# Experts stage: GpSimd starts a round's four result scatters only after the previous round's have landed

## The reference

```python
x = x + layernorm(attention(layernorm(x)))   # 16 heads of 8, relative position bias, softmax over 1024 keys
x = x + layernorm(ffn(layernorm(x)))         # mixture of experts
# ffn: 64 experts, 8 of them per token (best 4 of 8 groups first), capacity 128 tokens per expert
xe = zeros((E, CAP, H)).at[sorted_e, pos].set(tok_sorted, mode='drop')
h = silu(einsum('ech,efh->ecf', xe, w1)) * einsum('ech,efh->ecf', xe, w3)
ye = einsum('ecf,ehf->ech', h, w2)
out = segment_sum(vals * flat_w[:, None], flat_t, num_segments=T)     # dropped tokens count as 0
return out + silu(x @ shared_gate.T) * (x @ shared_up.T) @ shared_down.T
```

## Time and profile before

| | us |
|---|---|
| median of three runs | 1123.37 |
| the profiled execution, its own time | 1122.23 |
| its span, first to last instruction | 1120.4 |
| first result scatter starts | 959.79 |
| last result scatter starts | 1056.74 |
| first load of `finish` starts | 1064.77 |

### The profile page before, as it was taken

The page is one execution under the profiler, slowest core; times in us unless marked ns, Lnnn a source line. Parts: engine busy times, 40 slices in busy tenths (PEclk is TensorE's granted clock), DMA queues, the critical chain, the costliest instruction groups (busy, mean ns, idle before and its releaser), DMA issues. The chain is left out here.

```text
span 1120.4 us, 16485 instructions
## 1 busy us (share of the span) xinstructions
PE 911.1 (81%) x5190; PEld 289.5 (26%) x5190; DVE 816.9 (73%) x1314; ACT 685.9 (61%) x1416; POOL 555.9 (50%) x729
## 2 busy tenths in 40 slices
PE   5657999999999999999999999999986541745076
PEld 3311222222222222222222222222212321534043
DVE  6787888889889988988988998898841540322057
ACT  5714777777787777778778777777884210333113
POOL 6780020124356455645735554563576754456425
PEclk9867999999999999999999999999998665666578
DMA  5893432012332222222223212000222003410097
GB/s 140 262 250 63 118 80 62 15 38 47 83 110 87 90 90 55 59 49 82 82 91 104 49 39 50 5 6 14 79 82 91 2 3 90 119 51 13 17 400 275
DMA packets 107181, 96.35 MB, mean 86 GB/s; under 512 B 51406, under 2 KB 86512, under 8 KB 105046
## 3 DMA queue, kind: packets, MB, share of 16 engines
q1 hardware_dynamic: 89846, 88.12, 26.7%
q0 software_dynamic: 14336, 4.25, 1.8%
q10 hardware_dynamic: 2912, 2.93, 1.2%
HBM read 49.36 MB, written 65.24 MB: 102 GB/s over the span
## 5 line engine op out<-in xcount | busy, mean ns | idle before, releaser
L269 DVE TENSOR_REDUCE half_max<-s_pair 128x2 f32<-128x1024 f32 x512 | 602.0, 1218 | 77.8 <-PE s_pair L258 73.2
L1423 ACT ACTIVATE probs<-st_bank 128x512 f32<-128x512 f32 x1024 | 544.1, 602 | 170.3 <-PE st_bank L1519 157.2
L1285 POOL DMA_INDIRECT table<-rows,keys_i x256 | 255.5, 998 | 180.7 <-PE pv_bank L1528 67.5
L1519 PE MATMUL st_bank<-q_stack,k_stack 98*128 98x512 bf16 (+1 forms) x1024 | 324.0, 387 | 13.0 <-ACT probs L1423 4.9
L1528 PE MATMUL pv_bank<-probs,values 128*9 128x512 f32 x2048 | 267.7, 595 | 3.1 <-ACT unit_out L1358 2.8
L258 PE MATMUL s_pair<-k_stack,q_stack 64*128 64x512 bf16 x1024 | 202.5, 395 | 28.7 <-DVE half_max L269 26.4
L258 PEld LDWEIGHTS s_pair<-k_stack,q_stack 64*128 64x128 bf16 x1024 | 49.2, 93 | 344.3 <-issue 197.4
L1519 PEld LDWEIGHTS st_bank<-q_stack,k_stack 98*128 98x128 bf16 (+1 forms) x1024 | 77.7, 97 | 171.4 <-issue 86.2
L1721 POOL DMA_INDIRECT results<-out,ids x64 | 62.2, 971 | 53.7 <-ACT out L1783 37.3
L1754 DVE TENSOR_TENSOR h<-s_pair,gsig 128x256 f32<-128x256 f32 x16 | 6.8, 425 | 71.3 <-ACT gsig L1775 53.1
L1174 POOL CAST shift<-minus_max 128x16 bf16<-128x16 f32 x32 | 6.4, 201 | 101.2 <-DVE minus_max L275 101.1
(11 more groups left out here) (253 smaller groups left out, 845.9 us busy)
## 6 DMA issues: line engine op xcount, KB each, us to landing
results<-zeros SPq DMA_DIRECT2D x8, 2048.0 KB
choices<-results SPq DMA_DIRECT2D x6, 2048.0 KB, 23.7
table<-blank SPq DMA_DIRECT2D x8, 772.0 KB, 7.3
probs<-table SPq DMA_DIRECT2D x16, 386.0 KB
q_stack<-q_image SPq DMA_DIRECT2D x96, 64.0 KB
k_stack<-k_image SPq DMA_DIRECT2D x96, 64.0 KB
k_image<-k_piece SPq DMA_DIRECT2D x16, 256.0 KB, 3.3
table<-rows,keys_i POOLq DMA_INDIRECT x256
```

The costliest lines, as they stand in the source:

```text
L269: nc.vector.tensor_reduce(halves[:, h:HG:SIDE_HEADS, tile, half], stacks.s_pair[slot % S_SLOTS][:].rearrange("p (s k) -> p s k", s=SIDES), ...
L1285: pool.indirect_dma_start(out=table, out_offset=bass.IndirectOffsetOnAxis(ap=keys_i[c % 2][:, pick:pick + 1], axis=0), in_=rows[c % 2][:, ...
L1423: A.activation(probs[:, s % P_SLOTS, :], st_bank[at % ST_BANKS][:], ACT.Exp).then_inc(bank_free, 1)
L1519: M(bank(at)[:], k_stack[g][own, tile // PER, h, tile % PER * P:(tile % PER + 1) * P], q_stack[g][own, half, h, :], start=True, stop=True) ...
```

## The change

In GpSimd's loop, from the second round on, one wait is added ahead of the round's four scatters. Nothing else differs.

```diff
             for r in range(ROUNDS):
                 a = r % OUT_DEEP
                 pool.wait_ge(slot_read, 2 * (r + 1))
+                if r >= 1:
+
+                    put_of(pool, r - 1)
                 for q in range(Q):
                     pool.wait_ge(out_ready, r * Q + q + 1)
                     pool.indirect_dma_start(out=results, out_offset=bass.IndirectOffsetOnAxis(ap=ids[a][:, q:q + 1], axis=0),
```

## The result

| | before | after |
|---|---|---|
| median, us (4 runs each) | 1122.84 | 1134.23 |
| lowest to highest, us | 1121.2 to 1125.17 | 1133.35 to 1136.2 |
| ratio of the times | | 1.0107, 95% interval 1.0084 to 1.013 |
| span of the profiled execution | 1120.4 | 1131.5 |
| first scatter of round 0 starts | 959.79 | 960.58 |

The kernel became slower by 11.4 us. The span grew by 11.1: 10.5 of them between the two scatters (103.63 against 93.12), 0.8 ahead of the stage, and next to nothing behind it (`finish` takes 55.6 and 55.4 us).

A forecast was written before the change was run, and what follows sets the result against it. GpSimd's last landing was taken to set the block's end. Fifteen rounds x 6.83 = 102.4 us against 93.12 gave +9.3: 1131.5 us profiled, 1132.5 forecast for the median, 80% range 1128 to 1142.

The forecast's parts named there:

- What bounds: End of the experts block: GpSimd's last landing, drain, load and `finish` follow in series; a microsecond more there lengthens the kernel equally.
- The price of one wait, 3.00 us for a boundary: Between rounds on GpSimd: landing 2.15 plus restart and wait instruction 0.85 us, in place of 1.276.
- Table loads left out of the point value: Loads that delay fourth scatters' landings: nine left, none counted; if half cost 0.8 us each, 3.6 us more.
- The waits for results vanish behind the new ones: GpSimd's six idle times waiting for ACT's results, 16.6 us, are absorbed by the new waits.
- Every round starves: Rival: PE's results come one round at a time after each landing; +19 to +38 us, 1142 to 1162; 9%.
- six waits stay: Rival: results stay late, new waits paid at nine boundaries; +15.5 us, 1138.9 us; 13% including a mixture.

The follow-up runs named there:

- the second set: Later runs on another occasion, both kernels re-run with no edit: kernel before 1095.57 us, changed kernel 1124.98 us, ratio 1.0248.
- the second run of this kernel: The changed kernel run once more with no edit, against the kernel before: 1124.98 us, ratio 1.0248.
- the kernel with the third scatter: Against the kernel before: each round waits for the previous round's third scatter to land, each scatter for the one four back; 1108.43 us, ratio 1.0111.
- the kernel where SP waits: Last five rounds' landings waited for by SP in place of GpSimd, against the kernel before: ratio 0.9994.
- both runs with three back: Every scatter waits for the landing of the scatter three back, against the kernel before: ratio 1.0025; second run 1100.1 us.

## Why the prediction was right

The forecast was +9.3 us for the profiled execution; the span grew by 11.1 and the stretch by 10.5. The time of one wait was right for a reason that the experiments bear out. That the whole change cost no more than this took something that the forecast could not know: the pair was measured where PE's hand-offs were late, as in the trace it was made from. On a later occasion the same edit cost 27.5 us of the stretch, and the forecast had no case for that: so far the hit was luck.

- **What bounds.** Right. GpSimd's last landing, its drain and `finish` moved as one piece: 8.03 us from the last scatter's start to the first load before, 8.03 after.
- **The price of one wait, 3.00 us for a boundary.** Right in kind and nearly in size: thirteen of fifteen take 2.90 to 3.06, 2.91 in the middle. The landing has a row of its own in the second set, 2.2 us in the middle where 2.15 was put; so about 0.7 us are left for the restart, where 0.85 was put. The Trainium skill's price for a DMA from GpSimd (DMA: Bandwidth & Descriptors, Anatomy of one DMA) gives an estimate of 2.0 to 2.15 us here, close to the measured 2.2.
- **Table loads left out of the point value.** That is the 1.2 us between 102.4 and 103.63, and more: the first boundary is 1.52 us over 3.00 and the second 0.44; the other thirteen average 2.94 and give back 0.7. The prediction counted nine loads left when the stage starts; in its trace it was six, the other three having been issued between 950.0 and 958.8. In the changed kernel it is six too, issued at 963.09, 968.68, 971.58, 976.90, 983.34 and 990.09. The two long boundaries are those whose fourth scatter (964.41 and 972.76) starts 1.2 to 1.3 us after one of them; where the load was issued 3 us ahead or more, the boundary is as short as the rest. In the windows of the changed kernel (columns as in the earlier trace rows) a table load fills the DMA engines just when round 0's fourth scatter, started at 964.41, should land:

```profile
964.00:965.00 1.00, 0.29 (x6) 0.10 (x2) 0.00 (x0) 0.00 (x0) 0.70 (x2) 1.00 0.59 77
965.00:966.00 1.00, 0.00 (x0) 0.00 (x0) 0.00 (x0) 0.00 (x0) 0.38 (x1) 1.00 1.06 338
966.00:967.00 1.00, 0.00 (x0) 0.00 (x0) 0.21 (x1) 0.62 (x2) 0.00 (x0) 0.93 0.20 54
```

  At 338 GB/s and a DMA share of 1.06 the load leaves the scatter little room. No experiment took the loads away, so this rests on their coincidence in time, and it does not explain every late landing: the seventh boundary of the second run of this kernel (996.78) and one of the kernel with the third scatter (995.96) are long with no load in flight. The Trainium skill (DMA: Bandwidth & Descriptors, Issuing engines are not separate DMA queues) says that DMAs run on the same 16 DMA engines whichever engine issued them. That fits the late landing of 964.41; these traces do not show which DMA engine carried what.
- **The waits for results vanish behind the new ones.** Right for this pair: from the third boundary on all lie within 0.2 us of each other, and ACT's "remote" idling fell from 49.4 to 8.1 us. The reason that I gave is supported by the two traces (short groups of scatters, and a pause behind each) but was not put to a test, as no experiment met late hand-offs.
- **The chances.** "Every round starves" and "six waits stay" did not come. No rival asked what the change costs where the kernel before has no late hand-offs. By the prediction's own price that is 15 x (3.00 - 1.276) = 25.9 us; the second set shows 27.5 in the stretch, 2.5% of the time.

What remains open: why PE's results reached ACT late in the two traces of the first pair (by 3 to 11 us before, by about 3 us after) and in none of the twelve later ones, where no wait of ACT ends with "remote". In those two the scatter line has no row for the landing either, so some semaphore records are missing there; the word "remote" may come from that, but the idle times stand in the start times themselves. TensorE's clock does not explain it: the granted clock over the stretch is 0.68 in both traces of the first pair and 0.68 as well in the second run of the changed kernel, which has no late hand-off. The unprofiled runs of the first pair are as long as the profiled one, so it is not the profiler's doing. It did not come from the code alone, since the kernel before ran both ways. Of the 26.6 us between the two spans of the kernel before (1120.4 and 1093.8), 16.4 lie in the stretch and 9.9 ahead of it (first scatter at 959.79 and 949.86). Whether it is the chip or the occasion can't be told from these runs.

## What to carry to other kernels

On an engine that sends DMAs back to back and sets the end of its stage, a wait for the last one's landing costs the landing plus the restart less one interval, here 2.91 - 1.28 = 1.6 us, at each place where it holds. Here a wait for a landing at least four intervals back cost nothing measurable (0.0 and 0.1%), and one three back 0.25%, where single landings were late. Before a wait is called hidden, ask whether the idle time that hides it belongs to the code: here 16.6 us of it were there on one occasion and gone on another, and the same edit cost 1.1% and 2.5%. Where an engine ends a block with a drain, it is worth trying to let another engine wait for its last landings: here that gained 1.56 us in the trace, too little to show in the times.

## What the runs showed of the hardware

- GpSimd's drain at the end of the experts block takes 5.281 us in all thirteen traces where the landings were waited for first, and 5.3 us from the end of the last scatter where they were not (1034.88 + 0.97 = 1035.85 to 1020.56 + 20.58 = 1041.14 in the kernel where SP waits). Here it is a fixed piece of time and does not wait for landings.
- A scatter of 128 rows of 512 bytes costs GpSimd 0.97 us plus 0.30 us to the next whatever it writes: the last one moves some 65 KB in the slice 1058.0 to 1058.5 (131 GB/s for half a microsecond), while behind the one at 1047.81 the DMA engines move 2 GB/s in the slice 1049.0 to 1049.5 and 0 in the two beside it; all 64 take 969 to 973 ns. In nine of the later traces the longest scatter takes 1.04 to 1.11 us.
- The landing takes 2.1 us at least and 2.1 to 2.2 in the middle of each later trace, and 3.1 to 5.7 us at most. Where a late one held a wait, a table load had mostly been issued beside it. But in four traces (the second run of the changed kernel, the third scatter and both runs with three back) one is late near 996 us, 15 us or more behind the last load's issue, and nothing here says why.
- A clear of 128 x 1700 float32 on GpSimd takes 1.54 us; the 0.53 us of the trace's 128 x 512 one, times 3.3, would have given 1.76.
